# Indirect transfers in pairs, edges compared within 256 neighbours, and a reordered opening in a graph network on one core

## What is computed

```python
h = relu(layernorm(x));  x = x + attention(h)          # 16 heads, mask from the edges
h = relu(layernorm(x));  x = x + gated_rgcn(h)         # 8 relations, mean over edges of each type
h = relu(layernorm(x));  x = x + sage(sage(h))         # two layers, mean over incoming edges
h = relu(layernorm(x));  x = x + h @ W.T + bias        # W[src, dst] += edge weight

# the attention's mask, a table of 384 x 384
mask = full(-inf);  mask[src, dst] = softplus(etw)[edge_type_5 - 1];  diagonal filled
q, k, v = two chained linear layers each;  scores = q @ k.T * scale + mask;  softmax;  @ v;  @ wo.T
# relation r of the second layer, with counts[r][src, dst] = number of such edges
mean = counts[r].T @ h / max(counts[r].sum(0), 1);  out += mean @ weight[r]
```

## Time and profile before

| | us |
|---|---|
| median of 3 runs | 1020.36 |
| lowest, highest | 1017.2, 1020.98 |
| the profiled execution | 1019.42 |
| its span, first to last instruction | 1017.5 |
| PE busy in it | 943.4 |
| POOL busy in it | 488.1 |

### The profile page before, as it was taken

The page is one execution under the profiler, slowest core; times in us unless marked ns, Lnnn a source line. Parts: engine busy times, 40 slices in busy tenths (PEclk is TensorE's granted clock), DMA queues, the critical chain, the costliest instruction groups (busy, mean ns, idle before and its releaser), DMA issues.

```text
span 1017.5 us, 13970 instructions
## 1 busy us (share of the span) xinstructions
PE 943.4 (93%) x4743; PEld 843.1 (83%) x4743; DVE 610.8 (60%) x1039; ACT 366.9 (36%) x575; POOL 488.1 (48%) x411
## 2 busy tenths in 40 slices
PE   3999999994898979999999999999999959999994
PEld 2999999994797978888888888888888848887883
DVE  6888888862897344646455554564543764545625
ACT  5333333332785344322222232222322433334321
POOL 4133335774897343356475564754650843114312
PEclk9999999997999998999999999999999969999997
DMA  7976656521443526344534444343334413333301
GB/s 214 274 210 202 208 160 172 140 63 25 101 88 91 153 50 234 123 110 152 158 103 144 131 139 146 105 150 104 104 103 128 165 63 110 118 103 104 124 21 62
DMA packets 85783, 131.17 MB, mean 129 GB/s; under 512 B 22312, under 2 KB 63464, under 8 KB 85736
## 3 DMA queue, kind: packets, MB, share of 16 engines
q1 hardware_dynamic: 68800, 126.22, 39.5%
q0 software_dynamic: 15360, 0.08, 3.5%
q10 hardware_dynamic: 1576, 4.27, 1.3%
HBM read 116.65 MB, written 7.59 MB: 122 GB/s over the span
## 4 chain that ended last, share of the span: by engine, by line
PE 70%; DMA 17%; DVE 5%; issue 3%; POOL 3%; ACT 1%; ACTq 0%; DVEq 0%; POOLq 0%; SPq 0%
PE ps L570 49%; DMA mask_d<-type_val,cell 11%; PE ps L617 8%; DMA count_d<-met,cell 4%; PE ps L442 4%; PE ps L490 2%; PE ps L514 2%; PE ps L421 1%; PE ps L501 1%; POOL count_d L1452 1%; DVE stats L1015 1%; DMA b_in<-in_L_gnn_bo 1%; PE ps L721 1%; PE ps L479 1%; POOL mask_d L1440 1%
## 5 line engine op out<-in xcount | busy, mean ns | idle before, releaser
L1136 DVE TENSOR_TENSOR wlo<-raw,whi 128x1024 fp32r<-128x1024 f32 x120 | 203.1, 1696 | 130.5 <-ACT whi L827 130.3
L442 PE MATMUL ps<-acts,whi 128*128 128x384 f32 (+1 forms) x896 | 230.1, 338 | 4.3 <-DVE acts L1116 4.3
L1491 POOL TENSOR_TENSOR mean_lo<-mean_f,mean_hi 128x384 fp32r<-128x384 f32 x80 | 90.1, 1127 | 190.0 <-ACT mean_hi L926 189.9
L442 PEld LDWEIGHTS ps<-acts,whi 128*128 128x128 f32 x896 | 162.7, 190 | 4.5 <-issue 4.5
L442 PE MATMUL ps<-acts,wlo 128*128 128x384 f32 (+1 forms) x448 | 150.7, 336 | 0.0
L926 ACT ACTIVATE mean_hi<-mean_f 128x384 fp32r<-128x384 f32 x80 | 42.0, 525 | 298.1 <-DVE mean_f L1249 298.1
L570 PE MATMUL ps<-whi,mean_hi 128*128 128x512 f32 x480 | 149.0, 392 | 0.0
L570 PE MATMUL ps<-whi,mean_lo 128*128 128x512 f32 x480 | 147.8, 389 | 0.0
L570 PE MATMUL ps<-wlo,mean_hi 128*128 128x512 f32 x480 | 147.8, 389 | 0.0
L827 ACT ACTIVATE whi<-raw 128x1024 fp32r<-128x1024 f32 x120 | 125.5, 1048 | 17.5 <-PE ps L570 17.5
L570 PEld LDWEIGHTS ps<-wlo,mean_hi 128*128 128x128 f32 x480 | 90.2, 188 | 19.8
(11 more groups left out here) (155 smaller groups left out, 1510.9 us busy)
## 6 DMA issues: line engine op xcount, KB each, us to landing
raw<-in_L_gnn_weight SPq DMA_DIRECT2D x64, 512.0 KB, 3.3
rows_b<-rows_d SPq DMA_DIRECT2D x24, 384.0 KB, 4.8
raw<-in_L_gnn_w_gate SPq DMA_DIRECT2D x16, 512.0 KB, 3.3
raw<-in_L_gnn_W_self SPq DMA_DIRECT2D x16, 512.0 KB, 3.3
raw<-in_L_gnn_W_neigh SPq DMA_DIRECT2D x16, 512.0 KB, 3.3
count_d<-total_r SPq DMA_DIRECT2D x8, 576.0 KB, 4.5
rel_r<-count_d SPq DMA_DIRECT2D x8, 576.0 KB, 4.4
raw<-in_L_gnn_wq SPq DMA_DIRECT2D x32, 128.0 KB, 7.1
```

What stands on the lines that cost most here:

```text
L442: mm = pe.matmul(ps[:, j % 2, 0:N], stationary[j % RING][:, k, :], acts[:, a, moving, k, :], start=i == 0, stop=i == 3 * KT - 1)
L1136: dve.tensor_tensor(wlo_row[slot], raw[slot][:, :], whi_row[slot].bitcast(F32), ALU.subtract)\
L1491: pool.tensor_tensor(mean[1][:, k % 2, :], mean_f[:, k % 2, :], mean[0][:, k % 2, :].bitcast(F32), ALU.subtract).then_inc(S["mean_lo"], 1)
```

## The change

Semaphores of the scatters become two per table, for even and odd chunks, and a chunk waits only where it is the first of a pair (`GROUP = 2`), then for both of the pair before. So two transfers of one table are under way at once, and no cell may be in both: the compare runs over the pair's 256 neighbours, with `order` shifted by the chunk's place in it, and each chunk of a pair has spare cells of its own (`spare` is now a table, subtracted and added elementwise, and a cast makes the cell's integer). `LAG` is 38 and `LEFT` 8: 10 counts go in pairs between the last masks, 30 follow in pairs, 8 stand behind the first 8 heads, none after them. `sparse_w` goes; the weights' table is read into `mask`.

In the opening SP queues all of x before src and dst; ScalarE loads the edge types, then the table of the square root by an evaluation whose result is not read, then etw and the biases; Exp and Ln follow the rounding of h; the biases are turned behind h; GpSimd subtracts the low part of tile 0 in VectorE's place; VectorE's part of softplus and of the mask's diagonal moves behind the first tiles, and SP stores the mask's base ahead of tile 4 rather than tile 2.

```diff
-    LAG = 30
+    GROUP = 2
+    LAG = 38
+    LEFT = 8
...
-        order = sb("order", [P, P], F32)
-        same = sb("same", [P, 2, P], F32)
+        order = sb("order", [P, (2 * GROUP - 1) * P], F32)
+        same = sb("same", [P, 2, GROUP * P], F32)
...
+        def landed(eng, signals, c):
+            for q in range(GROUP):
+                need(eng, signals[q], 16 * ((c - q + GROUP - 1) // GROUP))
+
+        def others(c):
+            g = c // GROUP % (CHUNKS // GROUP)
+            return slice(GROUP * P * g, GROUP * P * (g + 1)), slice(P * (GROUP - 1 - c % GROUP),
+                                                                    P * (2 * GROUP - 1 - c % GROUP))
...  SyncE
-            sp_.dma_start(xres[:, 0, :], x_rows[:, 0, :]).then_inc(x_part[0], 16)
+            for nt in range(NT):
+                sp_.dma_start(xres[:, nt, :], x_rows[:, nt, :]).then_inc(x_part[nt], 16)
             for f, field in enumerate((src, dst)):
                 sp_.dma_start(e_in[:, f, :], field.rearrange("(c p) -> c p", p=P)).then_inc(S["edges_in"], 16)
-            for nt in range(1, NT):
-                sp_.dma_start(xres[:, nt, :], x_rows[:, nt, :]).then_inc(x_part[nt], 16)
...
                 if t == 2:
...
-                    sp_.wait_ge(S["mask_base_made"], 1 + NT)
-                    sp_.dma_start(plane(mask_d, 0), mask[:, :, :]).then_inc(S["mask_based"], 16)
                 if t == 4:
                     key_rows(2)
                     key_rows(3)
+                    sp_.wait_ge(S["mask_base_made"], 1 + NT)
+                    sp_.dma_start(plane(mask_d, 0), mask[:, :, :]).then_inc(S["mask_based"], 16)
...
-            sp_.wait_ge(S["mask_scattered"], 16 * EC)
+            landed(sp_, mask_scattered, EC)
...
-            sp_.dma_start(sparse_w[:, :, :], plane(weight_d, 0)).then_inc(S["weight_in"], 16)
+            sp_.dma_start(mask[:, :, :], plane(weight_d, 0)).then_inc(S["weight_in"], 16)
...  TensorE
-            pe.wait_ge(S["bcol_in"], 16 * 7)
-            pe.transpose(ps[:, 1, 0:7 * KT], b_in[:, :], ident[0:7 * KT, 0:7 * KT]).then_inc(S["edges_turned"], 1)
...  (behind the 24 transposes of h0)
+            pe.wait_ge(S["bcol_in"], 16 * 7)
+            pe.wait_ge(S["start_lo"], 1)
+            pe.transpose(ps[:, 2, 0:7 * KT], b_in[:, :], ident[0:7 * KT, 0:7 * KT]).then_inc(S["bcol_made"], 1)
...  ScalarE
+            act.wait_ge(S["ones_made"], 1)
+            act.activation(std[:, 0, :], epsc[:, :], ACT.Sqrt).then_inc(S["ones_made"], 1)
+            act.dma_start(etw_b[:, :], etw.partition_broadcast(P)).then_inc(S["etw_in"], 16)
...  VectorE
+                cols, later = others(c)
-                dve.scalar_tensor_tensor(same[:, n % 2, :], rows_b[:, s % RING, P * j:P * j + P],
-                                         e_col[:, KEY + f, c:c + 1], order[:, :], ALU.is_equal, ALU.mult,
+                dve.scalar_tensor_tensor(same[:, n % 2, :], rows_b[:, s % RING, cols],
+                                         e_col[:, KEY + f, c:c + 1], order[:, later], ALU.is_equal, ALU.mult,
...  GpSimd
+            pool.wait_ge(S["w_hi"], 1)
+            pool.tensor_tensor(wlo[0][:, :, :].rearrange("p f (c o) -> p f c o", c=4), wt_tiles[0],
+                               whi[0][:, :, :].bitcast(F32).rearrange("p f (c o) -> p f c o", c=4),
+                               ALU.subtract).then_inc(S["w_lo"], 1)
+            pool.wait_ge(S["sp_made"], 1)
...
-                need(pool, S["mask_scattered"], 16 * c)
+                if c % GROUP == 0:
+                    landed(pool, mask_scattered, c)
...
-            for c in range(EC):
-                scatter_mask(c)
+            for c in range(0, EC, GROUP):
+                for q in range(GROUP):
+                    scatter_mask(c + q)
                 if c >= LAG:
-                    add_counts(c - LAG)
+                    for q in range(GROUP):
+                        add_counts(c - LAG + q)
+            for c in range(EC - LAG, EC - LEFT):
+                add_counts(c)
...
             for i in range(H // 4):
                 for o in range(4):
                     normalise(i, o)
-                    add_counts(EC - LAG + i * 4 + o)
-            for c in range(EC - LAG + H, EC):
-                add_counts(c)
+                    if i * 4 + o < LEFT:
+                        add_counts(EC - LEFT + i * 4 + o)
```

142 lines of the change are left out of this document (73 added, 69 removed).

## The result

The changed kernel takes 1056.43 us, the median of 4 runs (1053.99 to 1056.85), against 1018.78 us for the kernel before, the median of 4 runs beside it (1014.95 to 1020.98). The ratio is 1.0348, with a 95% interval of 1.0318 to 1.0378. It is 37 us slower, where I forecast a time 3 us above that of the kernel before, and it lies outside my range.

The account below looks back on a forecast made before the run. Bound: GpSimd's scatter chain, one landing's latency at a time, ahead of its first normalisation. First heads +7.2 and other heads -4.2 gave +3 us on the median 1020.36: 1023.4 us, range 1006 to 1034, the likeliest's own 1015 to 1026.

Parts of the forecast that it names:

- nineteen pairs of masks alone: GpSimd's mask scatters before any count: 5.4 us per pair, bounds 5.0 and 5.9, 103 us in all, ending at 143.
- GpSimd is free at 260: GpSimd issues all work ahead of its first normalisation by 260 us; 243 with pairs at 5.0, 277 at 5.9.
- the five rounds: GpSimd alternating two masks and two counts: 6.4 us each by issue, plus three pieces of cells, 36 us, to 179.
- the fifteen pairs of counts: GpSimd's counts after the last mask: 5.9 us per pair, later 5.3, together 81 us.
- The opening: Reordered start: net gain 2 us, between 0 and 3, counted at nothing because GpSimd's chain sets the end.
- The mask wait: VectorE's 12.64 us wait at the first score for mask's read-back goes; mask in place near 217, wanted at 228.
- What is late next: TensorE waits from about 239 for GpSimd's first normalisation at 260; third at 268.7 instead of 261.44, 7.2 us late.
- The other heads: From third to last normalisation, 60.0 us before: 4.2 us saved through fewer cells, no late landing and lighter GpSimd.
- The compares: VectorE's compares over 256 neighbours: 0.27 us more per tile, free under 0.73 us of waiting; 13 us if uncovered.
- The line from release to end: Each microsecond of GpSimd's release moves the end by one from about 236 on: end = 1020.4 + (release - 257).
- The slower one: Rival: GpSimd late, pairs 0.3 us dearer, 12 us over 39 pairs, release 272, time 1035; 31%.
- The free second scatter: Rival: generation overlaps the first scatter's flight, a pair costs 4.1 to 4.6, 17 to 19 us faster, 1002; 15%.

Follow-up runs that it names:

- Opening alone: The changed kernel's reordered opening and wide compares, with single transfers and counts placed as in the kernel before: 1040.95 us, ratio 1.0211.
- opening of before: The changed kernel with the opening order of the kernel before; pairs, wide compares and the new placing of counts stay: 1046.68 us, ratio 1.027.
- edges first as well as the base ahead of tile 6: Two kernels: the changed one with both edits and counts placed as before, 1004.6 us; that one with no counts among the heads, 30 behind, 1030.51 us.
- wide compares alone: The kernel before with compares over 256 neighbours and the weights' table read into `mask`, nothing else: 1020.97 us, ratio 1.0039.
- base later: The changed kernel with SP's wait for the mask's base, and its store, ahead of tile 6 instead of tile 4: 1048.21 us, ratio 1.0284.
- spaced: The changed kernel with two memsets of a spare tile between the two stores of each pair of masks: 1075.87 us, one run.
- single: The changed kernel with every transfer waiting for the one before it on its table, counts placed as in the change: 1121.48 us, one run.

## Why the prediction was wrong

**The step that failed** is the term "nineteen pairs of masks alone: 19 x 5.4 = 103: GpSimd reaches the first count at 143", and with it "GpSimd is free at 260", whose upper bound of 277 was too low as well (by the prediction's own terms 5.9 throughout gives 275 and 5.0 gives 244, so its 277 and 243 are a little off). Measured: 168.22 - 42.43 = 125.8 us for the nineteen, and 295. The 35 us are made of the start (+2.4; 42.43 lies above my 41.5), the nineteen pairs (+22.8), the five rounds (43.2 for 36, +7.2) and the fifteen pairs of counts (83.6 for 81, +2.6). Everything that I built on the release held.

**The nineteen pairs.** Four stand in the stretch from 42 to 78 us and took 8.8 us each, 13.5 us over; the others some 6.05, 9.7 us over. I had priced all with the mean of thirty lone stores, in a kernel whose loads stood elsewhere. "Opening alone" showed stores without a partner landing as slowly in the same stretch (8.6 and 7.9 us), so in the start it was the landing that I had wrong, and not the pairing. In the middle, the time from a second store to the next pair was 4.70 us where a lone cycle is 4.06 to 4.17; between kernels it went from 4.26 to 4.83, and whether part of it comes from the second store being under way is open. My upper bound of 5.9 us per pair was nearly enough there.

**The opening** was "counted at nothing" because GpSimd's chain "starts no earlier". It starts later, at 42.4, and that was the smaller part. I had named SP's hold in front of tile 4's load and priced it at 1 us of TensorE; it cost TensorE nothing (no stall in the tiles). In the timeline of SP the base's store stands at 27.74 and tile 4's load right behind it at 28.23, where before the load stood at 21.79, so SP issues without a pause beside the first scatters. With the base ahead of tile 6 the time falls by 8 us (6.5 by the ratios), with the whole opening of before by 10 (8 by the ratios). What lengthens the landings is not settled. In the traces that give both for 40 to 60 us, mask stores are slow where the pieces of the weights are: 8.4 and 6.1 us in the change, 5.5 and 4.2 with the base ahead of tile 6, 4.5 and 4.2 with the opening of before, 3.4 and 2.9 in the kernel before. That fits loads bunched by SP's hold. But taking four stores of zeroes away brought no time, and with edges first as well as the base ahead of tile 6, where tile 4's load also goes early (19.98), the first four pairs took 31.0 and 35.2 us.

```profile
27.74 0.38 SPq L331 DMA_DIRECT2D mask_d<-mask  x1
28.23 4.31 SPq L312 DMA_DIRECT2D raw<-in_L_gnn_wq  x8
```

The 2 us for TensorE were wrong too: VectorE waited for the edge rows behind all of x, and the tiles began at 23.00, not 20.5; with the opening of before they begin between 21.78 and 23.36 in four traces, so the new one gained nothing that shows.

```profile
10.66 0.28 DVE L1057 SCALAR_TENSOR_TENSOR e_row<-e_in 48x128 f32<-48x128 int32 x1 [4.92 <-DMA e_in<-in_dst]
```

"Up to 1.5 us" was my price for this; queueing the edges first brought the relu from 11.78 to 7.71 us, and the time nothing.

**The five rounds** I priced by issue, and issue it was, but a dearer one. In the timeline GpSimd goes from one transfer to the next in 0.30 us nearly throughout:

```profile
186.56 1.53 POOL L1460 DMA_INDIRECT mask_d<-type_val,cell  x1 [0.30 <-issue]
188.40 1.60 POOL L1473 DMA_INDIRECT count_d<-met,cell  x1 [0.30 <-issue]
190.31 2.54 POOL L1473 DMA_INDIRECT count_d<-met,cell  x1 [0.30 <-issue]
193.15 0.99 POOL L1460 DMA_INDIRECT mask_d<-type_val,cell  x1 [0.30 <-issue]
194.45 1.97 POOL L1460 DMA_INDIRECT mask_d<-type_val,cell  x1 [0.30 <-issue]
```

The twenty issues add up to 31.7 us, where 0.98 and 1.56 each would make 25.4: several took 2.0 to 2.5 us. The wait for the last round's counts, 2.09 us, comes on top.

**The pairs of counts** were nearly right: 5.9 and in the quiet part 5.3 us expected, 5.6 measured there, 2.6 us too much over fifteen.

**The mask wait** was right: it went, and VectorE started the first score at 229.28 without waiting for it. **What is late next** was right in place (TensorE's ninefold turning, at 239) and in its pace: first to third normalisation 9.4 us for 8.7. **The other heads**: third to last 55.6 us, predicted 60.0 - 4.2 = 55.8. **The compares** were right, by "wide compares alone".

**The line from release to end**, end = 1020.4 + (release - 257), gives 1058.5 for the measured release of 295.1, and the kernel took 1056.4; for the other kernels with this placing it gives 1047.6 (opening of before, 1046.7 measured), 1051.8 (base later, 1048.2), 1077.4 (spaced, 1075.9) and 1125.0 (single, 1121.5). With sixteen counts behind the heads it gives 1034.2 and 1037.7 were measured, since the line leaves out what counts cost among the heads. From the opening of before to the single transfers, release moves by 77.5 us and the time by 74.8: as good as one for one.

**The rivals.** The slower one was the right sign with too little behind it: 0.3 us more per pair, where it was 1.2 on the masks. It "decides from a release of 262 on", under a tenth of a microsecond per pair above my price; with so thin a margin, and a start in a stretch that I had not looked at, 31% was too little. The free second scatter did not occur: the second store is issued some 1.4 us behind the first. The rule behind that rival, from the Trainium skill's "DMA: Bandwidth & Descriptors", section "Anatomy of one DMA — SWDGE (gpsimd) path" (some 2 us fixed, generation small), the trace does not bear out: 0.96 us of GpSimd per store is a quarter of a lone cycle, and from issue to landing a store took 3.4 us before and 8.4 us in the change (medians, 40 to 60 us).

The 14 counts behind the heads "hidden, nothing gained" was right as a price and blind as a comparison. What the change moved from there, and from among the heads, to the place ahead of them was 22 counts. Left at their old places, the same pairs run at 1007.6 and 1005.8 us.

## What to carry to other kernels

A queue of latency-bound work has a price for each place: ask of each item whether the engine has slack there. Here a count costs nothing behind the heads until the second layer wants it, 0.4 to 0.7 us among them and 2.8 us ahead of them, while the engines behind stand idle. And price a small transfer by the time it needs to land in the very stretch in which it will fly, with the loads that the changed kernel will have there, and not by a mean over the stage.

## What the runs showed of the hardware

A lone store of 128 cells takes from 2.4 us (52.29 to 54.68 in the timeline of the kernel before) to 8.6 us (42.22 to 50.80 with the new opening) until the next may go. The share of the queues is a poor measure of it: the first four pairs took 31.9 us at a share of 0.96 from 40 to 60 us, and 31.0 and 35.2 us in two traces at 1.11. The landing of the weights' pieces in the same stretch goes with it better, as above. With tile 4's load 8.9 us earlier, ahead of the wait for the base, the whole kernel took 8 us less (ratio 1.0284 for 1.0348). The issue itself varies too: 0.96 us for a store in most cases and 2.25 for the first, 1.55 and up to 2.54 for a count. A pair of counts takes 5.6 us for two even where the windows show 0 GB/s. And one trace is a thin base for the start: the same beginning gave four pairs in 34.5 to 36.9 us.
